# Self attentions of a decoder kernel: scores in row tiles of 32 for two heads at a time, transposes of normalised probabilities, output projection in three rounded products

## The reference

```python
q = split_heads(x @ q_out); k = split_heads(x @ k_out); v = split_heads(x @ v_out)
score = jnp.einsum('bhqd,bhkd->bhqk', q, k) / math.sqrt(d_head)
score = jnp.where(causal_mask, -jnp.inf, score)
weights = jax.nn.softmax(score, axis=-1)
ctx = jnp.einsum('bhqk,bhkd->bhqd', weights, v)
return ctx.transpose(0, 2, 1, 3).reshape(b, t, d) @ w_out
```

## Time and profile before

| | us |
|---|---|
| median of 3 runs | 3919.83 |
| lowest and highest | 3917.16, 3927.21 |
| span of the profiled execution | 3915.1 |
| its PE busy | 3308.1 (84%) |
| DVE, ACT, POOL busy | 1672.6 (43%), 1159.5 (30%), 238.9 (6%) |
| mean granted clock of PE | 0.943 |

### The profile page before, as it was taken

One profiled execution on the slowest core, in us unless ns is written; L12 is line 12 of the kernel. 1 busy time (PEld: TensorE's weight loads), 2 busy tenths in 40 slices (PEclk: granted clock), 3 DMA queues, 4 the chain that ended last, 5 costly groups with the idle time before them and its releaser, 6 DMA issues. The chain is left out here.

```text
span 3915.1 us, 45980 instructions
## 1 busy us (share of the span) xinstructions
PE 3308.1 (84%) x15122; PEld 1924.5 (49%) x15123; DVE 1672.6 (43%) x3287; ACT 1159.5 (30%) x3024; POOL 238.9 (6%) x205
## 2 busy tenths in 40 slices
PE   6999667788876699999788878999999998799894
PEld 5666412222221567777555545555665555444441
DVE  5666646666665212112166653333443333211113
ACT  2333224445444111111044433323343332211110
POOL 1000100000000200000100000000000001300002
PEclk9999879989898799999899999999999999999997
DMA  1000264444440300000100003000000000700323
GB/s 65 22 16 17 58 89 76 71 70 70 70 70 27 104 17 17 12 11 17 41 14 28 23 31 115 17 17 11 7 17 17 12 6 26 271 17 32 118 78 113
DMA packets 113094, 186.93 MB, mean 48 GB/s; under 512 B 8840, under 2 KB 53352, under 8 KB 112912
## 3 DMA queue, kind: packets, MB, share of 16 engines
q1 hardware_dynamic: 92032, 135.40, 14.3%
q0 software_dynamic: 7664, 27.40, 2.0%
q10 hardware_dynamic: 13216, 21.82, 1.6%
HBM read 130.10 MB, written 54.10 MB: 47 GB/s over the span
## 5 line engine op out<-in xcount | busy, mean ns | idle before, releaser
L1143 DVE TENSOR_REDUCE x_minus_max<-banks 128x2 f32<-128x1024 f32 x256 | 308.6, 1221 | 176.4 <-PE banks L1251 173.3
L1088 ACT ACTIVATE x_probs<-banks 128x512 f32<-128x512 f32 x512 | 290.9, 596 | 278.8 <-PE banks L1269 206.1
L1269 PE MATMUL banks<-x_stacked_q,x_stacked_k 105*128 105x512 bf16 x512 | 207.9, 416 | 83.0 <-ACT x_probs L1088 59.8
L476 ACT ACTIVATE a_probs<-banks,a_minus_max 128x128 f32<-128x128 f32 (+1 forms) x512 | 209.0, 426 | 145.0 <-DVE a_minus_max L559 143.3
L1984 PE MATMUL banks<-x_w_q,x_xT 128*128 128x512 f32 x512 | 232.6, 600 | 17.3 <-ACT x_xT L1856 17.3
L1251 PE MATMUL banks<-x_stacked_k,x_stacked_q 102*128 102x512 bf16 x512 | 171.5, 420 | 85.3 <-DMA x_stacked_k<-x_mask_parts_dram 60.5
L2090 PE MATMUL banks<-x_w_o,x_ctxT 128*128 128x512 f32 x512 | 221.0, 592 | 0.0
L1880 ACT ACTIVATE x_probs<-banks,x_minus_max,x_rroot 128x256 f32<-128x256 f32 x256 | 142.3, 560 | 204.1 <-DVE x_minus_max L1941 204.1
L1269 PEld LDWEIGHTS banks<-x_stacked_q,x_stacked_k 105*128 105x128 bf16 x512 | 50.4, 100 | 302.4 <-ACT x_probs L1088 194.0
L559 DVE TENSOR_REDUCE a_minus_max<-banks 128x2 f32<-128x512 f32 (+1 forms) x192 | 131.7, 686 | 82.3 <-PE banks L709 62.2
L2421 DVE TENSOR_TENSOR m_h<-banks,m_silu 128x512 f32<-128x512 f32 x39 | 27.0, 692 | 318.7 <-PE banks L2537 166.6
(11 more groups left out here) (347 smaller groups left out, 6431.9 us busy)
## 6 DMA issues: line engine op xcount, KB each, us to landing
x_parts_dram<-x_parts SPq DMA_DIRECT2D x16, 768.0 KB, 9.2
x_stacked_q<-x_parts_dram SPq DMA_DIRECT2D x48, 256.0 KB
x_stacked_k<-x_parts_dram SPq DMA_DIRECT2D x48, 256.0 KB
x_after<-a_z SPq DMA_DIRECT2D x16, 512.0 KB, 2.8
x_x<-x_after SPq DMA_DIRECT2D x16, 512.0 KB, 5.4
x_after<-x_z SPq DMA_DIRECT2D x16, 512.0 KB, 2.9
m_w<-in_m_g SPq DMA_DIRECT2D x8, 1024.0 KB, 5.7
m_w<-in_m_u SPq DMA_DIRECT2D x8, 1024.0 KB, 9.0
```

Source lines behind the costliest of these rows:

```text
L476: ins = act.activation(probs[:, n % 3, i * width:(i + 1) * width], psum[uses.bank(use)][:, i * width:(i + 1) * width], ACT.Exp, bias=minus ...
L1088: act.activation(probs[:, n % 8, :], psum[at.bank(f"exp{n}")], ACT.Exp, scale=SCALE)\
L1143: dve.tensor_reduce(minus_max[:, c % 2, h % 4, 2 * (n % 2):2 * (n % 2) + 2], at.pair(use), AX.X, ALU.max, negate=True)\
L1269: ins = pe.matmul(psum[at.bank(use)], stacked[1][u][:, h, s * P:(s + 1) * P], stacked[0][u][:, h, :], start=True, stop=True)
```

## The change

- Scores are made for two heads at a time. k is copied once (`kT`), without the zeros. A head's scores are a product over its own 32 rows of the array, at row position 0, 32, 64 or 96, and the two heads of a pair go to two banks. Each bank holds 384 columns: first block against first block (128), then second block against both (256). The mask product comes first now, and the score products add to it.
- There are 8 pairs in the loop instead of 12 units, the lag is 3 pairs. Scores have four banks as before, but a pair takes two of them.
- The reciprocals of the sums are taken for every pair, and POOL multiplies the probabilities with them in place (`normalise`), before PE transposes them. The spreading of reciprocals, their transposes, their copy and the scaling of the result are gone. Transposes use banks 4 and 5 together, a single set, and one copy takes both out.
- ACT rounds the value product (`round_ctx`) and DVE subtracts to get the rest (`rest_of_ctx`); both stages do so. The output projection of a1 takes three rounded products, so `w_o` of a1 is split at the stage's start, on DVE and POOL.
- The first scores wait for q and k, and v is waited for at the first value product. Banks of q, k, v and y are dealt anew. The memset of `k_of_head` on POOL is gone.

```diff
-UNITS = 12
+PAIRS_OF_HEADS = H // 2
 LAG = 3
+RING = 4
+SPAN = 3 * P
...
-        out = [(f"q0.{u}", 6), (f"q1.{u}", 7), (f"k0.{u}", 0), (f"k1.{u}", 1), (f"v0.{u}", 2), (f"v1.{u}", 3)]
+        out = [(f"q0.{u}", 0), (f"q1.{u}", 1), (f"k0.{u}", 2), (f"k1.{u}", 3), (f"v0.{u}", 6), (f"v1.{u}", 7)]
...
-            if n < UNITS:
-                out.append((f"S{n}.{u}", n % 4))
-            if LAG <= n < UNITS + LAG:
-                out.append((f"T{n - LAG}.{u}", 4 + n % 2))
+            if n < PAIRS_OF_HEADS:
+                out += [(f"S{n}_{i}.{u}", 2 * (n % 2) + i) for i in range(2)]
+            if LAG <= n < PAIRS_OF_HEADS + LAG:
+                out.append((f"T{n - LAG}.{u}", 4))
...
-        return out + low + [(f"y0.{u}", 4), (f"y1.{u}", 5)] + lowT
+        return out + low + [(f"y0.{u}", 6), (f"y1.{u}", 7)] + lowT
...
-            pool.memset(k_of_head[:, :, :], 0.0).then_inc(k_cleared, 1)
...
+            def normalise(b, p):
+
+                pool.wait_ge(inverse_ready, b * PAIRS_OF_HEADS + (p + 1))
+                pool.tensor_tensor(probs[:, p % RING, 0, 0:P], probs[:, p % RING, 0, 0:P],
+                                   inverse[:, p, 0, 0:1].broadcast_to([P, P]), ALU.mult)
+                for i in range(2):
+                    if i == 1:
+                        pool.tensor_scalar(probs[:, p % RING, i, 0:P], probs[:, p % RING, i, 0:P],
+                                           inverse[:, p, i, 0:1], None, ALU.mult)
+                    ins = pool.tensor_scalar(probs[:, p % RING, i, P:SPAN], probs[:, p % RING, i, P:SPAN],
+                                             inverse[:, p, i, 1:2], None, ALU.mult)
+                ins.then_inc(normalised, 1)
...
+                def exps(p):
+
+                    act.wait_ge(max_ready, b * PAIRS_OF_HEADS + (p + 1))
+                    if p >= RING:
+                        wait_full(act, f"T{p - RING}.{u}", turn)
+                    for i in range(2):
+                        use = f"S{p}_{i}.{u}"
+                        bank = psum[uses.bank(use)]
+                        act.activation(probs[:, p % RING, i, 0:P], bank[:, 0:P], ACT.Exp,
+                                       bias=minus_max[:, p, i, 0:1], accum_out=sums[:, p, i, 0:1])
+                        act.activation(probs[:, p % RING, i, P:SPAN], bank[:, P:SPAN], ACT.Exp,
+                                       bias=minus_max[:, p, i, 1:2], accum_out=sums[:, p, i, 1:2])\
+                            .then_inc(free[uses.bank(use)], 1)
...
+                def round_ctx(c):
+                    use = f"O{c}.{u}"
                     wait_full(act, use, turn)
+                    high_part_act(act, ctx_high[:, c, :], psum[uses.bank(use)][:, 0:T]).then_inc(ctx_rounded, 1)
...
-                    for i in range(4):
-                        rows = slice(DH * i, DH * i + DH)
-                        ins = dve.tensor_copy(k_of_head[rows, 8 * j + i:8 * j + i + 5:4, :],
-                                              psum[uses.bank(use)][rows, :].rearrange("p (c t) -> p c t", c=2))
-                    ins.then_inc(free[uses.bank(use)], 1)
...
+                    dve.tensor_copy(kT[:, 2 * j:2 * j + 2, :], psum[uses.bank(use)][:, :].rearrange("p (c t) -> p c t", c=2))\
+                        .then_inc(free[uses.bank(use)], 1)
+
+                def row_max(p):
+                    for i in range(2):
+                        wait_full(dve, f"S{p}_{i}.{u}", turn)
+                    banks = core.banks[:, 2 * (p % 2):2 * (p % 2) + 2, :]
+                    dve.tensor_reduce(minus_max[:, p, :, 0], banks[:, :, 0:P], AX.X, ALU.max, negate=True)
+                    dve.tensor_reduce(minus_max[:, p, :, 1], banks[:, :, P:SPAN], AX.X, ALU.max, negate=True).then_inc(max_ready, 1)
+
+                def invert(p):
+                    wait_free(dve, f"S{p}_1.{u}", turn)
+                    dve.reciprocal(inverse[:, p], sums[:, p]).then_inc(inverse_ready, 1)
...
+                    dve.tensor_copy(probsT[:, c % 2, 2 * j:2 * j + 2, :], core.banks[:, 4:6, 0:SPAN])\
                         .then_inc(free[uses.bank(use)], 1)
...
-                        for w in ("q0", "q1", "k0", "k1", "v0", "v1"):
+                def scores(p):
+                    c, j = p // 2, p % 2
+                    if p == 0:
+                        for w in ("q0", "q1", "k0", "k1"):
                             wait_free(pe, f"{w}.{u}", turn)
+                    for i in range(2):
+                        use = f"S{p}_{i}.{u}"
+                        wait_bank(pe, use, turn)
+                        pe.matmul(psum[uses.bank(use)][:, 0:SPAN].rearrange("p (k s) -> p k s", k=3)[:, 0:3:2, :], core.ident_bf[:, :],
+                                  core.causal[:, 0:2, :], start=True, stop=False, skip_group_check=True)
+                    for t in range(TT):
+                        for i in range(2):
+                            use, rows = f"S{p}_{i}.{u}", slice(DH * (2 * j + i), DH * (2 * j + i) + DH)
+                            ins = pe.matmul(psum[uses.bank(use)][:, 0:P] if t == 0 else psum[uses.bank(use)][:, P:SPAN],
+                                            qT[rows, c, t * P:(t + 1) * P], kT[rows, c, 0:(t + 1) * P],
+                                            start=False, stop=True, skip_group_check=True)
+                            if t == 1:
+                                done(ins, use)
...
+                def transposes(p):
+                    use = f"T{p}.{u}"
                     wait_bank(pe, use, turn)
+                    pe.wait_ge(normalised, b * PAIRS_OF_HEADS + (p + 1))
...
-                            ins = pe.matmul(psum[uses.bank(use)][:, :], ctxT[:, c, t * P:(t + 1) * P], w_o[:, c, :],
-                                            start=c == 0, stop=c == 3)
-                            continue
```

197 lines of the change are left out of this document (61 added, 136 removed).

## The result

The changed kernel takes 3952.3 us (median of 4 runs, 3945.2 to 3960.2) beside 3923.5 us for the kernel before in the same series (3917.2 to 3927.5). The ratio is 1.0076, with a 95% interval of 1.0055 to 1.0097: 0.76% slower, where 0.5% faster was predicted. The profiled execution of the changed kernel has a span of 3943.2 us against 3915.1 before, 28.1 more. One execution of the first experiment's kernel took 5081.8 us at a mean granted clock of 0.634 and is left out of its ratio.

The account below looks back on a forecast made before the run. No engine is full; order between engines ties the attention loop, plus PE waits and half clock. Per sequence a0 (first stage) +0.3, a1 (fourth) -2.5, each by 8: together -18, span 3915.1 to 3897, median 3902 us; range 3868 to 3938.

Parts of the forecast that it names:

- The k wait: Before a sequence's first scores: PE's wait for DVE's k copies goes, 3.3 us (fourth stage) and 0.7 (first).
- Scores: Score products on PE: eight instructions on 32 rows take 0.88 us, a pair 1.3 us, 8 pairs 10.3.
- Rival 3: Score products: row tiles don't run side by side, 1.28 us instead of 0.88 per pair, 3928 us; chance 0.12.
- Output projection: After the fourth stage's attention part: rounded products take 5.57 us instead of 6.87, 1.3 less; other PE work covers the last addend.
- The addition of the loop: Attention part, steps added in each engine's program order: last value products end at 27.5 us, 2.1 longer in the fourth stage.
- DVE no bound: DVE in the attention part: 17 us of work in all, against 17.4 (fourth stage) and 20 (first) before.
- Clock: PE gaps at the loop's start and end: half-clock loss of 1.8 us per sequence in both stages, 1.2 falls of 1.5.
- Rival 2: PE gaps at the loop's start and end: clock falls at both each time, 3.5 us instead of 1.8, 3929; chance 0.12.
- GpSimd: Normalising a pair on GpSimd: 1.6 us taken, ends 1.4 and 2.55, lying beside the other engines.
- the rival: Normalising in the loop: GpSimd becomes the bound, deciding from 2.5 us per pair; 3.0 gives 3966 us; chance 0.12.
- The sum: Both stages over 8 sequences: +2 us in the first, -20 in the fourth, together -18.
- Rival 1: Attention parts of all 16 sequences: the clock holds despite the gaps, 1.8 us off each, 3873 us; chance 0.17.

Follow-up runs that it names:

- the first experiment: Changed kernel with its three normalising products with a scalar per partition written as two-operand products, the scalar broadcast; ratio 1.0075 to the kernel before.

## Why the prediction was wrong

**The k wait, right.** -3.3 us and the half clock behind it: no idle time before the first scores in a1, and shortening that wait alone gives 33 of the 37 us that sharing the copies brings.

**Scores, right.** 0.86 us for the eight instructions where 0.88 was taken, a pair each 1.18 us apart where 1.3 was taken. Rival 3 (one after another) is out.

**Output projection, right in its size** (5.68 us instead of 6.87), and nobody waits for its addends.

**The addition of the loop, nearly right.** It gave 27.5 us for GpSimd at up to 2.1 us a pair. With GpSimd at 2.0 and no fall of the clock the part takes 26.8.

**DVE no bound, right** in the changed kernel. Its copies and PE's transposes take turns at the end of the loop, as counted: 1.05 us before the last value products.

**Clock, the step that failed.** I saw the gap before scores 2, called 1.7 us in the addition and 0.96 + 0.52 in the trace, and priced a fall at 1.5 us "every other time", later 1.2 falls a sequence. The price came from falls in the kernel before, and there it is about right: they last 3.4 us, and an attention part of a0 takes 28.2 us with one and 26.9 to 27.3 without. What I did not ask is what PE does while the clock is down. In the kernel before the scores go over full rows, in the new one over 32. The fall comes in every sequence, and lasts 13.7 us. Rival 2 had the right direction (it falls each time) and the wrong size for the same reason. What it costs is less than the 6.8 us of lost full-clock work, since the loop is bound elsewhere for part of it: filling the gaps gave back 0.0057 of the time, 22 us, or 1.4 us a sequence, with its own nine products and the falls that are left included. Why row-tiled scores keep the clock down stays open.

**GpSimd, the mis-sized term.** Taken 1.6 us a pair, ends 1.4 and 2.55; measured 2.75. The ends came from a select, which has no second operand, and from a long two-operand product. The product with one scalar per partition is like neither: 0.60 us for 128 and 0.92 for 256 columns, some 2.5 ns a column on 0.28 fixed. I had named the row's absence as a risk and given the rival 12 in 100. It decides from 2.5 us, I wrote, and once the clock is kept it does: between 2.55 (27.9 us) and 3.0 (31.5) the addition gives about 29.5 us for 2.75. With the start filled the 16 parts take 30.2 us on average, and with GpSimd at 2.0 us a pair 27.9, so the term is 2.3 us a sequence, 37 us in all (46 by the medians), but only where the clock is kept.

**The sum.** For a0 it said +2 us and 28.9 were measured, for a1 -20 and -1.5. In each of the 16 attention parts 2.3 us more than forecast (31.6 for 29.3) are 37 of these 45 us, and the first two sequences of a0, 8.5 us behind where two of the later ones lose 6.6, are 2 more. In a0 the prediction also had the kernel before too slow: 27.5 + 0.8 = 28.3 us for an attention part, where the eight take 27.7 on average, some 5 us in all. The rest, about 1 us, is not assigned. I had given slower 0.22, from causes taken one at a time; that two come together, each hiding the other, was in no rival.

**Two slips that changed little.** Rival 1 has the wait of 3.3 us make a fall "each time"; the first sequence of a1 has the wait (2.98 us) and no fall, so it is seven of eight. The chances named for "faster" (0.36, 0.17 and a quarter of 0.12) add to 0.56, not 0.58.

## What to carry over

- When a change takes buffers away at the head of a loop, the price of the gaps is not only their length. Look at what the engine runs behind them: with full-row scores the clock was back in 3.4 us here, with row-tiled scores in 13.7.
- Two causes can hide each other. The cheaper normalising gave nothing in the changed kernel and 46 us (1.0019 to 0.9901) once the gaps were filled. Before a cause is dropped because its cure does nothing, take away the other one as well.
- A large saving can be had by itself. Most of 37 us lay in one wait for DVE's copies, and moving four of the copies to ACT took them without touching the loop.

## What the runs showed of the hardware

GpSimd's product with one scalar per partition is dearer than the same product with the scalar broadcast as a second operand: 922 ns against 613 for 256 columns of f32, 601 against 398 for 128. The Trainium skill ("GPSIMD Engine Reference", 3.1 Elementwise) gives the two-input form as the one bound by the read port and so the slow one; here it is the fast one, and the measurement decides.

Adding PE work can make a kernel faster: nine products without effect per sequence took the ratio from 1.0076 to 1.0019, 22 us.

Row tiles of 32 rows for two heads at f32 do run side by side, eight instructions in 0.86 us, where the same eight over full rows take 1.31. Still open is why row-tiled products keep the clock down: the runs show it for f32 score products of 32 rows, two at a time, with six transposes a pair, and tried neither other row counts nor the loop without transposes. Nor is it known why the same gaps bring the clock down in 16 of 16 sequences of one kernel and in 10 of 16 of another.
